# A decoder layer on one core: POOL's product for scan step w waits for an operation of step w-3

## The reference, cut to what matters

```
u, z  = split(x @ in_proj.T);  u = silu(causal_conv(u))
dt, B, C = split(u @ x_proj.T)
delta = softplus(dt @ dt_proj.T + b);  A = -exp(A_log)
for each token t:                      # h: 512 channels x 16 states
    h = exp(delta[t] * A) * h + (delta[t] * u[t]) * B[t]
    y[t] = sum over states of h * C[t]
y = (y + u * D) * silu(z);  out = y @ out_proj.T
```

## Time and profile before

| | us |
|---|---|
| three executions | 1681.50, 1681.53, 1683.56; median 1681.53 |
| the profiled execution | 1688.74, of which the span is 1687.0 |
| the 128 scan steps lie at | 49.9 to 697.6 of the span |

### The profile page before, as it was taken

One profiled execution on the slowest core, in us unless ns is written; L12 is line 12 of the kernel. 1 busy time (PEld: TensorE's weight loads), 2 busy tenths in 40 slices (PEclk: granted clock), 3 DMA queues, 4 the chain that ended last, 5 costly groups with the idle time before them and its releaser, 6 DMA issues.

```text
span 1687.0 us, 15369 instructions
## 1 busy us (share of the span) xinstructions
PE 1370.0 (81%) x5571; PEld 646.2 (38%) x5571; DVE 815.6 (48%) x845; ACT 914.2 (54%) x1268; POOL 424.0 (25%) x290
## 2 busy tenths in 40 slices
PE   6566665789578966989633999999999987989999
PEld 2122222334223532555421222223223233558887
DVE  3899989996999799512722001001001015561001
ACT  4525542684258434402322999898998963760310
POOL 0645753674456556210530000000000001000000
PEclk9679887899879987969765999999999987989999
DMA  5323331332133323020599000000000000010801
GB/s 192 102 75 114 129 108 65 112 129 84 62 115 112 99 100 125 38 51 25 65 103 99 1 1 1 1 1 0 0 0 0 0 0 1 1 50 2 347 13 38
DMA packets 35631, 107.95 MB, mean 64 GB/s; under 512 B 3650, under 2 KB 14146, under 8 KB 32915
## 3 DMA queue, kind: packets, MB, share of 16 engines
q1 hardware_dynamic: 35572, 107.19, 22.9%
HBM read 93.60 MB, written 2.36 MB: 57 GB/s over the span
## 4 chain that ended last, share of the span: by engine, by line
PE 46%; DVE 24%; ACT 15%; issue 8%; DMA 5%; SPq 2%; POOL 0%; DVEq 0%; ACTq 0%; POOLq 0%
DVE ps L904 11%; PE ps L1591 9%; PE ps L1576 9%; ACT arena L739 6%; PE ps L1395 4%; PE ps L1700 3%; DVE arena L915 3%; DMA arena<-arena 3%; PE ps L1741 3%; PE ps L1350 3%; DVE arena L849 2%; ACT ps L595 2%; PE ps L1718 2%; PE ps L1281 2%; PE ps L1729 2%
## 5 line engine op out<-in xcount | busy, mean ns | idle before, releaser
L739 ACT ACTIVATE arena<-ps,bound 128x1024 f32<-128x1024 f32 (+1 forms) x416 | 421.0, 1215 | 25.9 <-PE ps L1576 25.9
L439 POOL TENSOR_TENSOR arena<-arena 128x1024 f32<-128x1024 f32 x128 | 327.1, 2556 | 236.7 <-DVE ps L904 190.0
L1350 PE MATMUL ps<-arena,ident 128*128 128x512 f32 x512 | 261.0, 651 | 67.1 <-DVE arena L915 67.0
L904 DVE TENSOR_TENSOR_SCAN ps<-ps,arena 128x1024 f32<-128x1024 f32 x128 | 300.7, 2350 | 25.7 <-ACT ps L595 15.5
L1576 PE MATMUL ps<-arena 97*128 (+3 forms) x832 | 218.3, 384 | 22.2 <-issue 20.1
L1591 PE MATMUL ps<-arena 128*32 128x512 f32 (+1 forms) x1664 | 222.5, 607 | 1.1 <-ACT arena L739 0.9
L595 ACT ACTIVATE ps<-arena 128x512 f32<-128x512 f32 x256 | 166.3, 682 | 71.1 <-DVE arena L915 67.2
L426 POOL TENSOR_TENSOR rstd<-ve,mhalf 128x4 f32<-128x4 f32 (+3 forms) x18 | 23.4, 1302 | 674.4 <-DVE ve L1199 468.4
L1174 DVE COPY arena<-ps 128x512 f32<-128x512 f32 x16 | 11.1, 692 | 354.3 <-PE ps L1591 354.3
L1350 PEld LDWEIGHTS ps<-arena,ident 128*128 128x128 f32 x512 | 100.5, 205 | 213.2 <-issue 113.2
L915 DVE TENSOR_TENSOR arena<-ps,arena 128x1024 f32<-128x1024 f32 x128 | 156.0, 1219 | 7.0 <-DVE ps L904 0.5
(11 more groups left out here) (182 smaller groups left out, 1505.9 us busy)
## 6 DMA issues: line engine op xcount, KB each, us to landing
arena<-bc_scratch SPq DMA_DIRECT2D x128, 512.0 KB, 3.7
arena<-in_mw SPq DMA_DIRECT2D x16, 1024.0 KB, 8.8
arena<-arena SPq DMA_DIRECT2D x48, 128.0 KB, 15.1
arena<-arena SPq DMA_DIRECT2D x12, 400.2 KB, 16.8
arena<-in_w SPq DMA_DIRECT2D x2, 1024.0 KB
out<-xt SPq DMA_DIRECT2D x4, 512.0 KB, 2.9
xt<-in_x SPq DMA_DIRECT2D x1, 1536.0 KB
arena<-in_ctx SPq DMA_DIRECT2D x1, 1200.8 KB, 7.7
```

Of the source, the lines that this page charges most:

```text
L439: pool.tensor_tensor(dbu[:, w % DR], du[:, DP * p:DP * p + DP], over(bg[:, w // BG % 2, n % BG], DP), ALU.mult).then_inc(S["dbu_ready"], 1)
L739: act.activation(flat(prob[0:n, v % 2, 2 * h:2 * h + 2]), ps[0:n, 2 * (r % 3):2 * (r % 3) + 2, :].rearrange("p a b -> p (a b)"), ACT.Exp, ...
L904: dve.tensor_tensor_scan(decay_banks(w), decay_banks(w), flat(dbu[:, w % DR]), carry[:, DP * p, n:n + 1], ALU.mult, ALU.add).then_inc(S["s ...
L1350: last = mm(bank(x), ident[:, :], state(2 * j + s)[:, x], start=False, stop=(j % HP == HP - 1 and (j in SUMMED or s == 1)))
```

## The change

One wait of POOL's `scan_input(w)` is on another semaphore. `scan_done` is raised by `scan(w-3)`, `hc_ready` by `times_c(w-3)`, which DVE runs later in the same step, behind `between`. Nothing else differs.

```
                 if w >= DR:
-                    pool.wait_ge(S["scan_done"], w - DR + 1)
+                    pool.wait_ge(S["hc_ready"], w - DR + 1)
                 pool.tensor_tensor(dbu[:, w % DR], du[:, DP * p:DP * p + DP], over(bg[:, w // BG % 2, n % BG], DP),
                                    ALU.mult).then_inc(S["dbu_ready"], 1)
```

## The result

| | before | changed |
|---|---|---|
| median of the executions, us | 1681.51 (1679.31 to 1683.56) | 1640.74 (1639.34 to 1641.98) |
| the profiled execution, us | 1688.74 | 1639.34 |
| the 128 scan steps, first scan to last product by C, us | 49.9 to 697.6: 647.8 | 49.5 to 652.6: 603.2 |
| from there to the end of the span, us | 989.4 | 984.9 |

The ratio is 0.9758, with a 95% interval of 0.9741 to 0.9774: 38 to 43.5 us less. Forecast were 1638.7 us and a gain of 42.8. In the two profiles the scan stretch alone is 44.6 us shorter. A second set of runs (e7_after_again) gave a median of 1644.18 against 1680.52: 36.3 us less, with 33 to 41 as its interval.

What follows compares the result with a forecast made beforehand. DVE was taken to bound the scan. Stalls of 52.2 us, 47.1 after what doesn't come back, less 4.3 of new cost gave a gain of 42.8 off 1681.53: 1638.7 us, range 1629.5 to 1655.

Steps and rivals of the forecast that it cites:

- The bound: Scan, 47 to 698 us: DVE, busy 596.95 of 651 us, sets the pace; POOL follows it step by step.
- What goes: DVE's SBUF-only operations beside POOL's product: 26 stalls of 2.0 us vanish, 52.2 us in sum.
- What doesn't come back: Stalls left at steps 4 and 113 (1.4, 0.2), losses to ACT (2.0, 0.8, 0.7); 47.1 us remain.
- rival (e): Whole kernel: nothing is absorbed and PE gets a higher clock; gain 53 or more, 1628 us; chance 0.04.
- What comes new: First operation of between waits 0.12 us for the product's end in 36 of 42 steps: 4.3 us lost.
- The rule that each loser stands for the whole overlap: Skill's exclusive port lock: single DVE operations lose the full 0.33 us, 11.9 in sum; time 1646.
- The added wait: POOL's later product release delays no scan (slack 4.3 us, was over 5) and keeps B's load distance.
- rival (c): B's loads: if one took over 8 us, pairs of steps would wait for POOL; +30, 1712 us; chance 0.03.
- (a): The collision moves: DVE pays 0.6 us in 36 steps; gain 25.5, time 1656 us; chance 0.09.
- (b): PE takes over: late out-projection loses the stalls of steps 10 to 12; gain 31, 1651 us; chance 0.09.
- (d): The release doesn't decide: POOL is late for other reasons, products start as now; 1681.5 us; chance 0.03.

Runs made afterwards that it cites:

- e7_after_again: The changed kernel once more, unaltered, for five rounds; 1644.18 us, ratio 0.978 to the kernel before.
- e8_conv_only: Kernel before with the later release only behind the convolution steps (i = 9 to 12 of chunks 0 to 2); 1658.19 us, ratio 0.9873.
- e1: Kernel before with the later release only where DVE's step three back has two or more SBUF-only operations (26 steps); 1638.79 us, ratio 0.9742.
- e2: Kernel before with the later release only in the other 99 steps, scan_done where DVE has two or more SBUF-only operations; 1685.52 us, ratio 1.002.
- e3_two_buffers: Changed kernel with two product buffers instead of three (DR = 2); 1643.00 us, ratio 0.9771.
- e9_issued: Kernel before plus a second wait of POOL's product, on a semaphore DVE raises between between(w) and the product by C; 1653.66 us, ratio 0.9829.

## Why the prediction was right

- *The bound.* DVE paced the scan: e8_conv_only and the pair e1 and e2 show stall for stall. Shown.
- *What goes* (26 stalls, 52.2 us). L849, L845, L877, L833, L938, L954 and L959 together are down by just that but for some 1.6 us that were left standing at steps 4 and 113 and the small cost at those that come first. At step 4 the four L833 take 2.72 us, where they took 4.74 and take 1.43 in steps 20 and 52: 1.3 us are left, with 1.4 forecast.
- *What doesn't come back* (3.5 us for ACT). DVE's new waits before scans are at step 54 (1.2 us; 2.0 foreseen with the earlier trace rows), step 25 (1.2; 0.8 foreseen as the loss behind step 20), steps 71 and 103 (0.4 and 0.3; 0.7 foreseen with the earlier trace rows) and step 57 (0.4, not foreseen). That is 3.4 us, close to the forecast. The total of DVE's idle time before scans didn't rise in the first pair of profiles, though (25.8 us, and 25.7 in the earlier trace rows): other waits, at steps 38 and 86, got shorter by 1.2 us each. At step 38 the reason is in the traces: ACT waits 5.55 us for PE's L1333 and not 6.78, as PE was granted 0.88 of its clock in the 14 us concerned and not 0.78, and its L1350 takes 3.60 us and not 4.67. In the second pair it is 0.83 and 0.80, and 3.71 and 4.57 us. At step 86 the second profile of before waits for 2.1 and not 2.9, so that most of it is chance. In that second pair the waits before scans did rise, by 2.5 us (26.9 against 24.4). So a bit of rival (e) was in it, at the size of a microsecond or two.
- *What comes new* (4.3 us in time, 42 x 0.12 = 5.0 in DVE's busy time). Measured some 5.4 in busy time, so the size is about right, but by two errors that cancel. Eleven of the 42 steps don't pay: their scan waited 0.3 us or more, so that the product is over when the first operation starts (L864: 1206 ns in six of seven). The other 31 lose 0.02 to 0.20 us each, about 4 us in all. And ten tiny operations that come first in a step and weren't counted lose 7 x 0.154 + 3 x 0.116 = 1.4 us.
- *The rule that each loser stands for the whole overlap* would have made it 11.9 us. What counts is when the operation gets going, in the rows 0.12 to 0.23 us before the product's recorded end.
- *The added wait.* Costs nothing. In e3_two_buffers the slack is down from 4.3 to 0.7 us by the prediction's own working, and no scan waits for it. The condition of rival (c), a load of over 8 us, didn't hold (4.0 us to landing in the changed kernel); its price was never tested.
- *Rivals (a), (b) and (d).* L859, L870 and L885 are up by 0.11 to 0.16 us and not by 0.6, which answers (a). DVE has no idle time before L928, and 20.0 us before L944 where it had 19.2, which answers (b). POOL's products are released by L915, which answers (d).
- *The size at the end.* 42.8 forecast. The scan gave 44.6 and 43.7 us in two pairs of profiles, 1 to 2 more than forecast, because the losses to ACT were partly made up elsewhere. The medians gave 40.8 and 36.3 in two comparisons. The runs differ from one set to the next by 3 us and more, and the part behind the scan by up to 5, so the medians can't confirm the last few microseconds: that 1640.74 lies as near to 1638.7 as it does is partly luck.

## What to carry to other kernels

Where a mean lies well above the median of the same form, look at what another engine was doing beside the long ones: two engines that each look fine in busy time can stop one another. A stricter wait on the engine that has slack can then be worth 2.4%, if it moves that engine's operation beside work that it doesn't meet (here a scan with its data in PSUM). Which steps need it can be read from the program: those in which the pacing engine has two or more of the operations concerned.

## What the runs showed of the hardware

- A POOL `tensor_tensor` of 128x1024 (2.35 us) and a DVE operation with two tensors from SBUF, or a fast `tensor_scalar`, don't run side by side: the one that comes second stands until the other is nearly done (L849 2.72 us instead of 0.75; the product 3.25 instead of 2.35 behind L885). A DVE `scan` or product with one input in PSUM runs beside it at full speed (2349 and 1219 ns).
- Against a POOL fill that only writes, DVE operations with two SBUF inputs run freely (752 ns), while `tensor_scalar` still waits for it (1.31 us instead of 0.52).
- In nearly every step of the kernel before with two or more such DVE operations, POOL's waiting product got in behind the first of them: the first is quick, and the second pays 2 us. The exceptions are step 4 (POOL was late and got in twice), step 74 (the third operation paid) and step 103 (the product stood 4.31 us, behind both of DVE's).
- A semaphore that DVE raises by an instruction of its own comes ahead of operations that were written before it and have no waits of their own: in e9_issued the product started 0.23 us after the first of four L939, while three were still to run.
